# Up biases carried as the last row of the expert weights, and the last group's routing spread over more tiles

## The reference, cut to what matters

```python
scores = softmax(xt @ gate_w.T)
_, idx = top_k(scores + gate_b, 2)            # two of 8 experts for each of 2048 tokens
def swiglu(x):
    g, l = x[..., ::2], x[..., 1::2]
    g = minimum(g, 7.0); l = clip(l, -7.0, 7.0)
    return g * sigmoid(1.702 * g) * (l + 1.0)
h = swiglu((xt @ w1[e] + b1[e]) * (xt @ w3[e] + b3[e]))   # 128 -> 512 -> 256
out += comb[:, e] * (h @ w2[e] + b2[e])                   # 256 -> 128
shared = swiglu((xt @ sw1 + sb1) * (xt @ sw3 + sb3)) @ sw2 + sb2
return layernorm(x + out + shared)
```

## Time and profile before

| | us |
|---|---|
| median of 3 runs (lowest 423.03, highest 425.62) | 423.24 |
| the profiled execution | 423.07 |
| its span, first to last instruction | 421.3 |
| PE busy | 347.6 |
| DVE busy | 281.5 |
| POOL busy | 194.0 |
| first turn with loaded rows (m = 7), start of PE's transposes | 261.47 |
| last placing of a tile's results | 397.86 |

### The profile page before, as it was taken

How to read it: one execution, slowest core, us unless ns; L and a number is a source line. 1 busy time by engine, 2 the same in 40 slices (tenths; PEclk the granted TensorE clock), 3 DMA queues, 4 the chain that set the end, 5 groups by cost and what they waited for, 6 DMA issues and landing times.

```text
span 421.3 us, 8518 instructions
## 1 busy us (share of the span) xinstructions
PE 347.6 (82%) x2415; PEld 224.6 (53%) x2415; DVE 281.5 (67%) x834; ACT 175.3 (42%) x498; POOL 194.0 (46%) x377
## 2 busy tenths in 40 slices
PE   2637887888988879798967998978799999999880
PEld 1224466666656658576656554534455555555450
DVE  3435477777878897869876867987466666666322
ACT  2212344444534443344532344344355555555313
POOL 9700022224222558722474434357755656565323
PEclk9999999998999998969998799999899999999996
DMA  4764544766654732310003001113211111110063
GB/s 100 171 212 128 178 141 120 210 202 172 186 157 132 201 98 63 104 34 11 27 28 119 14 13 44 33 39 92 63 45 44 47 45 45 40 50 19 26 201 100
DMA packets 53197, 39.56 MB, mean 94 GB/s; under 512 B 7623, under 2 KB 46632, under 8 KB 53147
## 3 DMA queue, kind: packets, MB, share of 16 engines
q1 hardware_dynamic: 50881, 34.33, 29.3%
q0 software_dynamic: 2272, 4.69, 3.3%
HBM read 26.05 MB, written 12.69 MB: 92 GB/s over the span
## 4 chain that ended last, share of the span: by engine, by line
PE 42%; DVE 23%; issue 10%; POOL 9%; DMA 6%; SPq 5%; ACT 2%; ACTq 0%; POOLq 0%; DVEq 0%
PE pT L1491 7%; PE pS L1491 6%; DVE negmax L934 4%; PE pM L1502 4%; POOL xs L633 3%; PE pM L1297 3%; DVE inv_den L950 2%; POOL rstd L613 2%; PE pO L1482 2%; PE pT L1321 2%; PE pT L1492 2%; PE pS L1311 2%; PE pS L1492 2%; PE pO L1334 2%; DVE X L1004 1%
## 5 line engine op out<-in xcount | busy, mean ns | idle before, releaser
L711 POOL DMA_INDIRECT ys<-sim_rhs,row_dest x39 | 40.5, 1039 | 43.3 <-ACT sim_rhs L868 41.7
L766 ACT ACTIVATE PT<-pT 128x512 f32<-128x512 f32 x64 | 38.0, 594 | 33.3 <-PE pT L1321 29.9
L1491 PE MATMUL pT<-W,XH 128*128 (+1 forms) x94 | 51.7, 632 | 0.0
L934 DVE TENSOR_REDUCE negmax<-pS 128x4 f32<-128x512 f32 x64 | 43.4, 679 | 9.6 <-PE pS L1311 9.2
L1071 DVE TENSOR_TENSOR PT<-pT,PT 128x512 f32<-128x512 f32 x47 | 32.4, 689 | 25.9 <-PE pT L1492 17.7
L1491 PE MATMUL pS<-W,XH 128*128 (+1 forms) x94 | 49.3, 607 | 0.0
L611 POOL TENSOR_SCALAR vareps<-meanvar 128x1 f32<-128x1 f32 x32 | 8.4, 263 | 86.1 <-DVE meanvar L963 85.8
L1311 PE MATMUL pS<-Kdiag,Qst 128*128 128x512 f32 x64 | 40.4, 638 | 6.3 <-DMA Kdiag<-parts_scr 4.7
L852 ACT COPY XH<-pO 128x384 f32<-128x384 f32 x47 | 22.4, 478 | 49.4 <-PE pO L1484 45.7
L1502 PEld LDWEIGHTS pM<-W,XH 128*128 128x128 f32 x188 | 28.1, 191 | 21.0 <-issue 17.4
L633 POOL DMA_INDIRECT xs<-X,slot x32 | 33.2, 1036 | 8.1 <-issue 5.8
(11 more groups left out here) (264 smaller groups left out, 828.1 us busy)
## 6 DMA issues: line engine op xcount, KB each, us to landing
parts_scr<-qk_hi SPq DMA_DIRECT2D x16, 256.0 KB, 2.9
W<-in_L_ffn_w SPq DMA_DIRECT2D x16, 256.0 KB, 3.9
Qst<-parts_scr SPq DMA_DIRECT2D x32, 96.0 KB
Kdiag<-parts_scr SPq DMA_DIRECT2D x64, 48.0 KB
Kst<-parts_scr SPq DMA_DIRECT2D x32, 96.0 KB
Qdiag<-parts_scr SPq DMA_DIRECT2D x64, 48.0 KB
sim_add<-xs SPq DMA_DIRECT2D x39, 65.0 KB
parts_scr<-qk_lo SPq DMA_DIRECT2D x8, 256.0 KB, 3.0
```

Of the source, the lines that this page charges most:

```text
L711: pool.indirect_dma_start(ys.ap(), bass.IndirectOffsetOnAxis(ap=row_dest[:, k:k + 1], axis=0), YO[:, i % RING, :], None).then_inc(s_ysc[i ...
L766: act.activation(PT[:, u % 3, :], pT[:, 0, :], ACT.Exp, scale=SCALE).then_inc(p_sb, 1)
L934: dve.tensor_reduce(out=negmax[:, b % 2, HG * j:HG * (j + 1)], in_=pS[:, u % 2, :].rearrange("p (g k) -> p g k", g=HG), axis=AX.X, op=ALU.max,
L1491: pe.matmul(bank, XH[:, 1 - p, 2 * P:3 * P], W[:, bass.ds(e_up * I2, I2)], start=True, stop=False)
```

## The change

**Bias as a weight row.** Each token row gets a constant 1.0 behind its 128 values (column D of X2, set once), and so has 131 columns. The expert phase transposes columns 1 to 128: features 1 to 127 and the constant. W1 and W3 hold rows 1 to 127 of the weights in partitions 0 to 126, and the bias in partition 127. Since feature 0 is minus the sum of the others, row 0 of the weights is subtracted from each other row: SP loads it, repeated over 127 partitions, into `first_rows_of` (two more DMAs of 254 KB for an expert), and POOL subtracts it, one 127x512 operation for each of 18 matrices, in the slots of LESS_SLOTS (16 and 17, then 24 and 25, 29 and 30, ..., 59 and 60). The weight loads move to slots 13, 21, 26, ..., 56; each waits for the subtractions of the one before. The gate weights get the same on DVE (128 columns, once). The 94 bias products of 512 columns go, the DMAs that built `bias3` and the memsets of it too, and the shared expert's bias scalars. The down bias stays a product, of three rows instead of 128.

**Buffers.** XH shares its memory with `first_rows_of`, so that ACT waits at slot 66 for all subtractions; `lin_g`, `hidT[1]` and `x2_of` get memory of their own, by which the last two experts' weights need not come late.

**Last group.** Routing steps go to turns 6 to 13, one in most; the counts to turn 11; `late_tiles` and `tile_table` are cut in four pieces at turns 14 to 17; the eight scatters go one or two after each of `place(3)` to `place(8)`.

```diff
-PAD_LOAD = 9
-LAST_ROUTING = {6: (0,), 7: (1, 2), 8: (3, 4), 9: (5,), 10: (6, 7), 11: (8,)}
-LAST_COUNT, LAST_TILES, LAST_TABLE = 10, 12, 13
+PAD_LOAD = 11
+LAST_ROUTING = {6: (0,), 7: (1,), 8: (2,), 9: (3,), 10: (4, 5), 11: (6,), 12: (7,), 13: (8,)}
+LAST_COUNT, LAST_TILES = 11, 14
+LAST_SCATTER = {3: (0, 1), 4: (2,), 5: (3,), 6: (4, 5), 7: (6,), 8: (7,)}
-XW = D + 2
+XW = D + 3
-UP_SLOTS = {**{15 + 4 * e: e for e in range(E - 2)}, 67: E - 2, 68: E - 1}
+UP_SLOTS = {13: E, **{21 + 5 * e: e for e in range(E)}}
+LESS_SLOTS = {n + 3 + k: (e, k) for n, e in UP_SLOTS.items() for k in range(2)}
...
-            def up_weights(e, done):
-                a, c = (w1[e], w3[e]) if e < E else (sw1, sw3)
-                sp.dma_start(W1[:, e * I2:(e + 1) * I2], a).then_inc(done, 16)
-                sp.dma_start(W3[:, e * I2:(e + 1) * I2], c).then_inc(done, 16)
+            def up_weights(e):
+                i = LESS_ORDER[e]
+                if i:
+                    sp.wait_ge(w_less, 2 * i)
+                for k, (W, w) in enumerate(((W1, w1 if e < E else sw1), (W3, w3 if e < E else sw3))):
+                    first = e * D * I2 if e < E else 0
+                    sp.dma_start(W[0:P - 1, e * I2:(e + 1) * I2],
+                                 bass.AP(w.tensor, first + I2, [[I2, P - 1], [1, I2]])).then_inc(s_w_up, 16)
+                    sp.dma_start(first_rows_of[0:P - 1, k, :], bass.AP(w.tensor, first, [[0, P - 1], [1, I2]])).then_inc(s_w_up, 16)
...
+                if n in LESS_SLOTS:
+                    e, k = LESS_SLOTS[n]
+                    here = (W1, W3)[k][0:P - 1, e * I2:(e + 1) * I2]
+                    pool.wait_ge(s_w_up, 64 * (LESS_ORDER[e] + 1))
+                    pool.tensor_tensor(here, here, first_rows_of[0:P - 1, k, :], ALU.subtract).then_inc(w_less, 1)
...
-                if i in (1, 3):
-                    for k in range(G4):
-                        scatter(NG - 1, (i // 2) * G4 + k)
+                for k in LAST_SCATTER.get(i, ()):
+                    scatter(NG - 1, k)
...
-                    pe.matmul(bank, XH[:, 1 - p, 2 * P:3 * P], W[:, bass.ds(e_up * I2, I2)], start=True, stop=False)
-                    pe.matmul(bank, bias_rows[:, k, :], bias3[:, bass.ds(e_up * I2, I2)], start=False,
+                    pe.matmul(bank, XH[:, 1 - p, 2 * P:3 * P], W[:, bass.ds(e_up * I2, I2)], start=True,
                               stop=True).then_inc(done, 1)
...
-                    pe.matmul(pM[:, 0:D], bias_rows[:, 2, :], bias3[:, bass.ds(e_y * D, D)], start=False,
+                    pe.matmul(pM[:, 0:D], three[:], b2_parts[:, bass.ds(e_y * D, D)], start=False,
                               stop=True).then_inc(y_ps, 1)
```

More of the change, by code:

```diff
@@ L91, in decoder_layer @@
         ones = sb("ones", [P, P])
-        bias_rows = sb("bias_rows", [P, 3, P], BF16)
+        three = sb("three", [3, P], BF16)
         head_ones = sb("head_ones", [P, U, 32])
@@ L802, in shared_up @@
                 elif step == 0:
-                    if g == 0 and c == 0:
-                        act.wait_ge(s_bcol, 32)
-                    else:
+                    if g or c:
                         act.wait_ge(f_hid, 2 * g + c)
                     act.wait_ge(f_ps, done + 1)
-                    act.activation(lin_g, pT[:, 1, :], ACT.Identity, bias=b1_col[:, c, 0:1], scale=1.0).then_inc(f_out, 1)
+                    act.copy(lin_g, pT[:, 1, :]).then_inc(f_out, 1)
                 elif step == 2:
@@ L814, in shared_up @@
                     act.wait_ge(f_ps, done + 1)
-                    act.activation(lin_l, pT[:, 1, :], ACT.Identity, bias=b1_col[:, c, 1:2], scale=1.0).then_inc(f_out, 1)
+                    act.copy(lin_l, pT[:, 1, :]).then_inc(f_out, 1)
             def copy_logits(b):
@@ L1462, in shared @@
                                       stop=False)
-                        mm = pe.matmul(here, bias_rows[:, 2, :], bias3[:, E * D:(E + 1) * D], start=False, stop=True)
+                        mm = pe.matmul(here, three[:], b2_parts[:, E * D:(E + 1) * D], start=False, stop=True)
                     mm.then_inc(f_ps, 1)
```

147 lines of the change are left out of this document (69 added, 78 removed).

## The result

The changed kernel takes **732.14 us** (median of 4, 729.9 to 733.49), the kernel before 424.12 us on the same chip (median of 4, 423.03 to 425.62): a ratio of 1.726, 95% interval 1.7196 to 1.7324. Forecast were 411.2 us, with 404.0 to 419.5 as the range. The profiled execution has a span of 731.6 us, 310.3 more than before.

What follows compares the result with a forecast made beforehand. It took PE to bound steady expert turns, DVE turns 8 to 14, the batch-to-batch chain attention. 423.07 - 9.5 - 0.3 - 7.1 + 0.8 - 0.5 + 4.5 + 0.2 = 411.2 us, range 404 to 419.5.

Steps and rivals of the forecast that it cites:

- the small parts: Minor costs across the kernel: gate weights' subtraction 0.2 us; added DMAs, shorter bias work and shared expert's copies charged nothing.
- Its rival, 0.8 us for each of nine bursts: Attention: weight bursts delay the score operands behind them in SP's queue, each holding PE 0.8 us; 418.4 us, chance 0.10.
- The removed products, -9.8: Expert turns without the two up-bias products: 9.5 us gained over 26 turns, 0.3 for the last two or three.
- The loop of 2.67: Steady expert turns: PE's tile, DVE's hidden values, then PE's transposes of them limit a turn to 2.67 us, not 2.61.
- the stall: DVE's 3.60 us of idleness before turn 17's product, taken not to return; its return a rival, 415.5 us, chance 0.12.
- The turn in the changed kernel, 2.67: Steady expert turn, from turn 19 to 45: falls from 3.034 to 2.67 us, a gain of 0.364 each.
- Its rival of a longer DVE loop: Expert turns: POOL's placing falls on DVE's clipping, so a turn takes 2.85 us, not 2.67; 415.9 us, chance 0.11.
- Turns 8 to 19: Expert turns paced by DVE: turn 19 starts at 300.9 against 308.04, 7.1 us gained, half of it one stall.
- Late scatters, +0.8: Last group: second table's first rows arrive at 312.2, PE wants them in turn 23 at 311.5; 0.8 us lost.
- Turns -1 to 6, -0.5: First expert turns, holding the last two batches' chains: 0.5 us gained, taken between 0 and 3.4.
- Gate weights, +0.2: Slot -11: the gate weights' subtraction adds a link before PE's transposes, 0.2 us lost.
- Eighteen subtractions, +4.5: POOL's subtractions delay DVE 10.5 us, less than half reaching the end: 4.5 us lost, ends 0 and 21.4.
- the lock of the first rival: POOL's port lock shared with DVE: each subtraction delays the chain by its whole length; 428.1 us, chance 0.04.

Runs made afterwards that it cites:

- split version: The changed kernel with each 127-row weight load cut into 112 and 15 rows and the repeated row 0 loaded over 128 partitions: 438.28 us, ratio 1.0296.
- e15: The split version with one-column subtractions and fewer loads in a burst, row 0 repeated over 128 partitions: 420.41 us, ratio 0.9985.
- e16: The kernel e15 with row 0 repeated over 16 partitions instead of 128, the one-column subtraction over as many: 416.8 us, ratio 0.9893.

## Why the prediction was wrong

**The step that failed** stands under the small parts: "18 more DMAs of 254 KB make bursts of 1 MB: the DMA engines are busy 0.17 of 160 to 200 us, so I charge nothing". The sum had 0 where 295 us belonged. The reasoning took 254 KB to be as quick as the 256 KB of before, spread over sixteen engines, and looked only at how idle these were. Nothing in the trace of before could show a load of 127 partitions, and the term was not bounded from both sides as the other unseen costs were. What the runs showed in its place: each such load runs on one DMA engine, lasts about 10 us and holds SP's queue as long. Its rival, 0.8 us for each of nine bursts, had the mechanism (Kdiag behind the weights in SP's queue) and a price one fortieth of the true one.

Even with the loads mended the sum is wrong: 411.2 forecast, 438.28 for the split version. By its own terms:

- **The removed products, -9.8: right.** Alone they give -13.5 us by the ratio. The loop of 2.67 was 2.695, and turns 19 to 45 fell by 8.8 us where 9.5 was forecast. The rest is mostly in turns 8 to 19, which took 36.98 us and not 42.93, without the stall.
- **The turn in the changed kernel, 2.67: missed, some 6 us.** The prediction counted the two products that go and took the third, the down bias's, as unchanged; the diff puts it on 3 rows. 27 turns by 0.21 are 5.7 us; the ratios say 7.4. Its rival of a longer DVE loop had a turn of 2.85 for another reason: PE's own products set it, not the loop.
- **Turns 8 to 19: right.** Forecast 33.9 us from turn 8 to 18 and 36.6 to turn 19, measured 33.30 and 36.62. That the stall goes was a guess, half of the forecast gain, and it came true by luck: the split version has it again as soon as the routing goes back to its old turns (3.7 us), and no run says why.
- **Late scatters, +0.8 (312.2 - 311.5 is 0.7): not there.** After, PE's only wait of over 1 us for loaded rows in the expert phase is that of turn 7, the first that has any.
- **Turns -1 to 6, -0.5: about right for turns 1 to 8**, 24.08 us in the split version and 23.95 without bias products, against 24.84 (24.80 in the changed kernel). But slot 60 to turn 1 takes 3.2 us more in the split version, where nothing was forecast; this is not explained. The subtractions are not its cause: without them it is 31.79 us, before 29.27.
- **Gate weights, +0.2:** too small to be seen; from the start to slot 0 one kernel differs by 0.4 from profile to profile.
- **Eighteen subtractions, +4.5: mis-sized, 10.5 us.** DVE's delay was set at 10.5 us and is 15.15; nine of the eighteen were taken to be mostly alone at 0.3, while fifteen of the eighteen hold up a DVE instruction, mostly by 1.0. And of the delay not "less than half" but 10.5 / 15.15, some 70%, reaches the end, the effect on PE's clock included. 10.5 lies in the middle between my two ends; the mechanism is the lock of the first rival, and the halvings of the earlier trace rows, half as long, were the wrong neighbour. The earlier trace rows was also read too simply: DVE's scaling starts there 0.79 us before POOL's addition, while POOL's scatter of 236.12 to 237.22 us was running, so the addition can be charged at most its own 1.19 us, and not all of the scaling's delay.
- **Bursts, even over sixteen engines: not nothing.** Slots 16 to 28 take 9 to 10 us more. The mean DMA share of 0.17 was read in another stretch, 160 to 200 us; in slots 16 to 28 of the kernel before it is 0.69.

The chances suffered from the same fault: 0.03 for slower, since each rival changed one term, and none asked whether a new transfer has the shape of the old ones.

## What to carry to other kernels

Price each new DMA by its own shape, not by its bytes: here 127 partitions put 254 KB on one engine, and SP could not issue what stood behind. Read DMA load in the stretch where the transfer starts, for the operand behind it matters, not the mean. When a change moves work onto POOL, look for each DVE instruction that will run beside it, and cut POOL's work into short instructions; and take every changed operand shape on PE as a change, even where it has fewer rows. And compare versions that differ by 1% within one set of runs only.

## What the runs showed of the hardware

- A DMA of 254 KB over 127 partitions used one of sixteen engines (share 0.07), at 26 GB/s; with two of them under way SP's issue of the next took 10.12 us.
- A weight load of 3 rows did not start under the product before it, nor the next load under its own product: a turn of 2.91 us against 2.70 with 128 rows.
- In a burst of weight loads the operand issued last was awaited 4.6 us after its issue with the repeated row over 128 partitions (e15), 2.5 us with it over 16 (e16), 1.5 us in the kernel before.
- A DVE instruction of 0.35 us beside a POOL subtraction of 1.27 us took 1.28; four subtractions of 128 columns, 1.7 us together, cut the sum of such delays from 15.15 to 3.83 us.
- PE stood still at 84 to 86 us of the split version, and the granted clock was 0.50, the lower level of 1.2 GHz, at 92 to 94 us, after PE had been busy 5.83 of the 6 us between. The score product after the stall of 4.46 us took 0.76 us, that after the stall of 2.05 us in e15 0.47.
- A stall of DVE put down to "remote" sits in one turn of four kernels with the old routing: the kernel before (3.60 us), the two with its loads cut at 127 (3.60) and at 124 (3.52), and the split version with the old routing (3.50). It is absent from a fifth with the old routing, the kernel before without the up-bias products. Nothing here explains it.
